# The edge part of the first graph layer, computed for two node tiles at a time

## The reference

```
sums = jax.ops.segment_sum(edge_attr, src, num_segments=n)
counts = jax.ops.segment_sum(jnp.ones((edge_attr.shape[0],), edge_attr.dtype), src, num_segments=n)
edge_attr_agg = sums / jnp.maximum(counts, 1.0)[:, None]
combined = jnp.concatenate([x, edge_attr_agg, u_expanded], axis=1)
h = jax.nn.relu(combined @ W1 + b1)
return h @ W2 + b2
```

## Time and profile before

| | before |
|---|---|
| median of 3 runs | 950.42 us (949.53 to 958.12) |
| profiled execution, its own time | 953.29 us |
| span of its trace | 951.5 us |
| granted TensorE clock, mean of the span | 0.938 |
| PE busy, share of the span | 91% |
| DVE busy | 68% |
| ACT busy | 44% |
| POOL busy | 75% |
| the graph-layer loop in the span | about 712 to 801 us |

### The profile page before, as it was taken

One profiled execution on the slowest core, in us unless ns is written; L12 is line 12 of the kernel. 1 busy time (PEld: TensorE's weight loads), 2 busy tenths in 40 slices (PEclk: granted clock), 3 DMA queues, 4 the chain that ended last, 5 costly groups with the idle time before them and its releaser, 6 DMA issues.

```text
span 951.5 us, 20339 instructions
## 1 busy us (share of the span) xinstructions
PE 862.1 (91%) x6492; PEld 533.4 (56%) x6492; DVE 644.7 (68%) x2267; ACT 421.6 (44%) x1156; POOL 710.7 (75%) x498
## 2 busy tenths in 40 slices
PE   3899997987999999999999999999959996599994
PEld 1444443444554554554454655555548986499993
DVE  4799998999487556566565566465876888645552
ACT  3555645333354333344343334334314555166663
POOL 3778888888888888888888888878732156677875
PEclk8699998897899899999999999999979998599997
DMA  9966675446556455445554555653586454578885
GB/s 292 233 121 114 101 154 96 64 44 107 96 98 107 44 85 86 64 52 77 97 85 68 87 102 87 129 86 35 74 238 208 140 191 147 177 124 133 136 135 56
DMA packets 149267, 108.72 MB, mean 114 GB/s; under 512 B 105223, under 2 KB 137162, under 8 KB 149036
## 3 DMA queue, kind: packets, MB, share of 16 engines
q0 software_dynamic: 61344, 26.21, 30.2%
q1 hardware_dynamic: 81312, 70.49, 26.3%
q10 hardware_dynamic: 6508, 10.73, 3.2%
HBM read 65.07 MB, written 42.45 MB: 113 GB/s over the span
## 4 chain that ended last, share of the span: by engine, by line
PE 51%; POOL 17%; DVE 17%; issue 7%; DMA 5%; ACT 1%; SPq 0%; DVEq 0%; POOLq 0%; ACTq 0%
POOL edge_sums L755 17%; PE ps L1423 8%; DVE r2t L1751 6%; PE ps L1647 5%; PE ps L1636 5%; PE ps L1212 5%; PE ps L1259 3%; PE ps L1250 3%; PE ps L1564 3%; PE ps L1359 2%; DVE same L1691 2%; PE ps L1373 2%; DMA edge_sums<-sums,addr 2%; PE ps L1308 2%; PE ps L1280 1%
## 5 line engine op out<-in xcount | busy, mean ns | idle before, releaser
L755 POOL DMA_INDIRECT edge_sums<-sums,addr x352 | 552.9, 1571 | 129.5 <-issue 99.8
L1788 DVE TENSOR_SCALAR oh<-node,dsrc 128x500 bf16<-128x500 int16 (+1 forms) x448 | 134.5, 362 | 71.4 <-PE ps L1423 70.7
L1423 PE MATMUL ps<-oh,r2t 128*64 128x500 bf16 (+1 forms) x1344 | 146.6, 362 | 1.4 <-DVE oh L1788 1.4
L1010 ACT ACTIVATE r<-ps 128x500 f32<-128x500 f32 (+1 forms) x224 | 103.5, 550 | 80.1 <-PE ps L1359 79.8
L1423 PEld LDWEIGHTS ps<-oh,r2t 128*64 128x64 bf16 x1344 | 70.6, 111 | 72.8 <-issue 33.7
L1751 DVE TENSOR_TENSOR r2t<-ps,r 125x4096 f32<-125x4096 f32 x25 | 110.3, 4412 | 0.0
L800 POOL DMA_INDIRECT out_x<-r x56 | 88.1, 1572 | 27.2 <-DVE r L2188 10.6
L1212 PE MATMUL ps<-edges,same 128*128 128x65 f32 x704 | 98.5, 286 | 10.4 <-ACT sums L829 4.7
L1212 PEld LDWEIGHTS ps<-edges,same 128*128 128x128 f32 x704 | 89.3, 199 | 32.6 <-issue 30.1
L1691 DVE SCALAR_TENSOR_TENSOR same<-srow,src_f,below 128x128 f32<-128x128 int32 x352 | 101.0, 343 | 1.9 <-DMA srow<-in_src_row 1.8
L829 ACT ACTIVATE sums<-ps 128x260 f32<-128x260 f32 x88 | 35.0, 399 | 138.5 <-PE ps L1212 138.5
(11 more groups left out here) (300 smaller groups left out, 1381.0 us busy)
## 6 DMA issues: line engine op xcount, KB each, us to landing
srow<-in_src_row SPq DMA_DIRECT2D x44, 512.0 KB, 6.0
edges<-in_edge_attr SPq DMA_DIRECT2D x22, 512.0 KB
r<-routed_rows SPq DMA_DIRECT2D x56, 129.0 KB
r<-hpre_rows SPq DMA_DIRECT2D x12, 500.0 KB, 4.4
edge_sums<-sums,addr POOLq DMA_INDIRECT x352, 3.3
r2t<-in_ew SPq DMA_DIRECT2D x4, 1024.0 KB, 11.5
hpre_rows<-r ACTq DMA_DIRECT2D x16, 250.0 KB, 2.1
edge_sums<-r SPq DMA_DIRECT2D x4, 884.0 KB, 13.4
```

The lines of the kernel that those rows point to most:

```text
L755: pool.indirect_dma_start(out=tables[k], out_offset=bass.IndirectOffsetOnAxis(ap=addr[:, j:j + 1], axis=0), in_=sums[:, j % OR, :], in_off ...
L1010: act.activation(phT[:, R % 2, h, 0:n], bank(BP[h], 128, 0, n), ACT.Square).then_inc(pair_squares, 1)
L1423: m = mm(ps[EA * a:EA * (a + 1), BD * BANK:BD * BANK + n], lhsT=parts3[:, (DCH - 1 - 2 * w // DW) * DW + (2 * w + a) % DW, s, :], rhs=oh[: ...
L1788: v.tensor_scalar(oh[:, (2 * i + a) % OHS, 0:nt * P].rearrange("p (t n) -> p t n", t=nt), node16[:, 0:nt, :], dsrc[:, 2 * w + a:2 * w + a ...
```

## The change

The edge part is computed for two tiles at once, in the even turns only: four products of 250 columns in place of twice four of 125. Pieces 0 and 1 go into bank 1, pieces 2 and 3 into bank 2, so that a pair fills both banks, and `ha(t)` now waits for `hsum_ready >= t`, the sum of tile t-1, the last to read the pair before. The sum stays one instruction per tile; it reads its 125 columns of each of the four pieces out of both banks. The last tile, 24, is alone and keeps products of 125 columns.

```diff
-            def ha(t, u):
-                if not inside(t):
-                    return
-                if t <= 1:
-                    wait(pe, aggT_ready, NBK if t else 1)
-                wait(pe, hsum_ready, t - 1)
+            def ha(t):
+                if t % 2 or not inside(t):
+                    return
+                if t <= 2:
+                    wait(pe, aggT_ready, (NBK if t else 1))
+                wait(pe, hsum_ready, t)
+                n = (min(t + 2, T) - t) * P
                 for m in range(MC):
-                    z = mm(bank(1 + u, 128, m * P, (m + 1) * P), lhsT=w1a[:, m * 128:(m + 1) * 128], rhs=aggT[:, bass.ds(t * P, P)],
+                    c0 = (1 + m // 2) * BANK + m % 2 * 2 * P
+                    z = mm(ps[:, c0:c0 + n], lhsT=w1a[:, m * 128:(m + 1) * 128], rhs=aggT[:, t * P:t * P + n],
                            start=True, stop=True)
                 z.then_inc(ha_ps, 1)
...
             def hsum(t, u, k):
                 if not inside(t):
                     return
-                wait(v, ha_ps, t + 1)
+                wait(v, ha_ps, t // 2 + 1)
                 wait(v, hpre_back[k % 2], k // 2 * 16 + 16)
                 wait(v, gnn_ps, t - 1)
-                v.tensor_tensor(hs[:, u, :].rearrange("p (m n) -> p m n", m=MC), bank(1 + u, 128, 0, MC * P).rearrange("p (m n) -> p m n", m=MC),
-                                hpre2[:, k % 2, :, u * P:(u + 1) * P], ALU.add).then_inc(hsum_ready, 1)
+                pair = ps[:, BANK:3 * BANK].rearrange("p (a c) -> p a c", a=2)[:, :, 0:4 * P].rearrange("p a (j n) -> p a j n", j=2)
+                v.tensor_tensor(hs[:, u, :].rearrange("p (a j n) -> p a j n", a=2, j=2), pair[:, :, :, u * P:(u + 1) * P],
+                                hpre2[:, k % 2, :, u * P:(u + 1) * P].rearrange("p (a j) n -> p a j n", a=2), ALU.add).then_inc(hsum_ready, 1)
```

More of the change, by code:

```diff
@@ L1586, in gnn @@
             def gnn(t, u, k):
-                ha(t, u)
+                ha(t)
                 layer2(t - 1, 1 - u)
```

## The result

The changed kernel takes 954.56 us (median of 21 runs, 951.98 to 957.93) where the kernel before takes 951.19 (21 runs beside them): ratio 1.0038, 95% interval 1.0023 to 1.0054, so 2.2 to 5.1 us longer. A second measurement (6 runs, beside 29 of before at 951.23) gave 957.53 us, ratio 1.0072, interval 1.0045 to 1.01. It moved the way that was forecast, by about twice the forecast 1.7 us, and in the second measurement by 6.3 us.

A forecast was written before the change was run, and what follows sets the result against it. PE bounds ordinary turns, DVE's routing the stretches between. Walking both put x2 of tile 22 1.58 us late; with 0.1 for the load, +1.7 us: median 952.1 us, own range 951.3 to 953.2, wider range 949.6 to 954.6.

The forecast's parts named there:

- the gain of the ordinary turns: Edge products on PE: each pair saves 0.26 us, 12 pairs 3.1 us, if PE alone decided.
- The stalls: PE ahead of the pairs of tiles 14, 20 and 22, waiting for DVE's sum: 0.72, 0.84 and 1.02 us.
- the walk: Loop followed turn by turn through PE and DVE from tile 4: x2 of tile 22 comes 1.58 us late.
- Rival one: Pairs' banks come free in time, PE's saving passes whole: 947.3 us; chance 0.13.
- rival two: DVE's routing sets the pace, lateness recovers in batch three, nothing moves: 950.4 to 950.8 us; chance 0.13.
- Rival three: Pair's 250 columns cost as much as twice 125, 1.94 us, adding 2.3 us: 954.4 us; chance 0.10.
- The loop's start: Before tile 4's sum: its load moves by 0 to 0.17 us, taken as 0.1; all else there is early.
- term H: Time a pair's four products of 250 columns hold PE, taken as 1.68 us.

The follow-up runs named there:

- r4: Fourth trace of the unmodified changed kernel, no edit: loop 90.14 us, against 85.74 us in the first trace of before.
- e4: Changed kernel plus four products of 250 columns that nobody reads behind the first pair: 955.88 us, ratio 1.0047.
- e2: Changed kernel with pairs for tiles 0 to 3 only, single tiles with a bank each from tile 4 on: 953.08 us, ratio 1.0023.
- e9: Changed kernel with fourteen products that nobody reads put into PE's idle places of the loop: 953.11 us, ratio 1.0029.
- e1: Changed kernel with tiles 0 to 3 taken one by one as before, pairs from tile 4 on: 955.97 us, ratio 1.0049.
- e5: Changed kernel's order, banks and waits, but each pair in eight products of 125 columns instead of four of 250: 960.58 us, ratio 1.0102.

## Why the prediction was wrong in size

**What held.** The mechanism stands: the pair waits for the sum of the tile just before, it stands whole in front of layer 2 behind a ranking, the gain of the ordinary turns is lost there, and the third batch doesn't recover. The stalls were put at 0.72, 0.84 and 1.02 us and stand in the rows as 0.54, 0.66 and 0.84. Most of the 0.18 is the way of counting: the walk counts from when PE could start the next group, 0.35 us after the router's start (731.57 - 731.22), and the row's idle time from the end of the router's row, 0.50 after it. Counted as in the walk, the first stall is 759.75 - 758.71 - 0.35 = 0.69. The sum kept its 0.67 us, and the load for tile 4 its time. Rival one fell with these stalls, rival two with x2 of tile 19, which did not recover (56.15 us behind layer 2 of tile 4, before 53.49). Rival three as it was put, pairs at 1.94, fell with 1.77; but two turns save only 0.10 of the 0.26 us, as the second step below shows, so it came nearer to the walk than the forecast did. That its 954.4 lies next to 954.56 is luck: it has neither the start nor the clock in it.

**The step "The loop's start" failed.** It took 0.1 us and bounded it by 0.17. Layer 2 of tile 4 came 1.81 us later from the loop's start. I looked only at the load for tile 4 and took all else before 725.65 as early. The first pair lengthens PE's wait for the first relu from 0.65 us (first row of the fence below) to 1.48; the clock fell behind it, 1.6 us (39.60 against the 38.00 of r4 and 38.01 of e4). The rest is the start in series: pair 4 waits for sum 3, 0.15 us. Where the clock stays up, the start costs little beside a late load: with it landing 13.5 to 13.6 us after the first edge product, as in the first trace of before (37.55), the first part takes 37.86 when single tiles follow (e2). With an early load it costs 1.36 when pairs follow (e4 and e9 at 38.01, against 36.65 in e1; the loads landed 12.4 to 12.5 us after that product).

**The walk's term H was mis-sized.** 1.68 us is right only behind layer 2. Behind the router's products a pair holds PE for 1.77, and layer 2 there for 731.00 - 729.19 = 1.81 in place of 1.73. Before, this 0.08 lay inside the 0.97 of each narrow edge part, and I took it away twice with the narrow parts and gave it back nowhere. Odd turns now start with layer 2, which pays it. So two turns save 2 x 0.97 + 2 x 1.73 - 1.77 - 1.73 - 1.81 = 0.09, measured 0.10, not 0.26. From layer 2 of tile 4 on, x2 of tile 8 stands 0.21 us earlier than before in place of 0.50, x2 of tile 9 already 0.22 later in place of 0.16 earlier, and the gap to the walk grows to 0.99 by tile 19 (56.15 against 782.20 - 727.04 = 55.16). The walk gave x2 of tile 22 at 66.08 (64.50 + 1.58); it stands at 796.20 - 729.19 = 67.01. The lateness there is 2.51 instead of 1.58.

**What no step held: the clock.** The longer waits of PE let the granted clock fall to 0.50 in one or two stretches of each traced execution, 1.3 to 2.7 us each, 2.7 us a trace in the mean (1.60; 1.85 and 2.71; 1.67 and 1.31; 1.68). The trace of before had it, behind the loop, where PE waits for DVE's last tiles (its timeline of PE, then its busy times by window there):

```profile
714.75 1.99 PE L1564 MATMUL ps<-w2s,r 128*125 128x256 f32 x8 [0.65 <-ACT r L1113]
...
799.76 0.43 PE L1574 MATMUL ps<-ident,r 125*128 125x125 f32 x2 [1.50 <-DVE r L2009]
...
801.76 0.43 PE L1574 MATMUL ps<-ident,r 125*128 125x125 f32 x2 [1.24 <-DVE r L2009]
...
803.65 0.64 PE L1598 MATMUL ps<-r,upper 125*125 125x40 f32 x2 [1.11 <-DVE r L2054]
```

```profile
800.00:806.00 6.00, 3.57 (x22) 3.29 (x20) 4.26 (x25) 3.85 (x8) 4.77 (x5) 0.78 0.59 202
```

The ranking's first product takes 0.44 us at full clock, and 0.64 here. A change that adds waits of 0.7 to 1 us to PE should have had a rival with that price.

**The sum, corrected.** Against the first trace of before, without falls: 0.45 to the first ranking (38.00 against 37.55), 0.90, 1.94, -0.57, that is 2.7 us; with the falls 4.3 to 7.3 in the four traces. Against the second trace of before, whose load came earlier (36.69), all of these are 0.85 more. The timed runs gave 2.2 to 5.1 and, the second time, 4.3 to 9.5. The split of the timed difference between the two causes isn't settled, since only traced executions show where the clock fell. From layer 2 of tile 4 on, the 2.5 us without falls are 1.1 for the banks and 1.4 for the pair between ranking and layer 2.

The Trainium skill (Perfetto Trace Analysis, section Matmuls) says that larger matmuls are more efficient and that independent groups should rotate through PSUM banks. These runs agree with both, at 0.10 us a pair for the first and 1.1 us for the second, and here the second weighs more.

## What to carry to other kernels

Before products are merged, see in the rows what the first group behind each neighbour takes more than the same group elsewhere, and which group pays that afterwards. Where two engines take turns as the bound, ask what the merged work now stands in front of at the places where the other engine leads. And count PE's new idle times: each can cost more by the clock behind it than by itself.

## What the runs showed of the hardware

The granted clock fell to 0.50 at or behind idle times of PE of 0.72 to 1.48 us, not each time and not at the same place in two executions of one kernel; a fall made a group of products of 256 columns last up to 3.67 us instead of 1.9 to 2.0 and cost the loop 1.3 to 2.8 us. It came with products of 125 columns (e5) as with wider ones. With these places filled by useless products there was none in two traces. The first group of products behind the router's two of 8 columns holds PE 0.08 to 0.09 us longer than the same group behind wide ones.
